# Two stages and a prologue: maxima taken in an earlier stage, and loads put in another order

## What is computed

```python
xn = layernorm(x)
q, k, v = rope(proj(xn, W_q)), rope(proj(xn, W_k)), proj(xn, W_v)
scores = einsum('bhnd,bhmd->bhnm', q, k) / sqrt(8)
attn = softmax(where(causal, scores, -inf), axis=-1)
s = einsum('bhnm,bhmd->bhnd', attn, v) -> (b, s, 128) @ W_o
g = silu(ffn(xn))                   # gelu(xn @ W1' + b1) @ W2' + b2
x = x + s * g
xn = layernorm(x)
x = x + retention(xn) * silu(mixture_of_experts(xn))
```

## Time and profile before

| what | us |
|---|---|
| median of 3 runs (1002.06 to 1005.51) | 1004.39 |
| the profiled execution, its own time | 999.11 |
| its span | 997.3 |
| first stage | 0 to 118.6 |
| attention's prologue | 118.6 to 149.4 |
| attention's loop | 149.4 to about 541 |
| between the layers | about 541 to 645 |
| retention, routing, experts | about 645 to 997 |

### The profile page before, as it was taken

One profiled execution on the slowest core, in us unless ns is written; L12 is line 12 of the kernel. 1 busy time (PEld: TensorE's weight loads), 2 busy tenths in 40 slices (PEclk: granted clock), 3 DMA queues, 4 the chain that ended last, 5 costly groups with the idle time before them and its releaser, 6 DMA issues. The chain is left out here.

```text
span 997.3 us, 25279 instructions
## 1 busy us (share of the span) xinstructions
PE 869.6 (87%) x9413; PEld 467.9 (47%) x9414; DVE 801.1 (80%) x1691; ACT 726.1 (73%) x1493; POOL 290.6 (29%) x335
## 2 busy tenths in 40 slices
PE   3999899999999999999988699888899999889960
PEld 3666544333334333333334577643444444468850
DVE  6665499999999999999942565399999999928895
ACT  2656408888888888888866445488999999948851
POOL 4875311111111000000012657600444443005560
PEclk9999959999999999999989799969999999979985
DMA  5579861644444353332005678596555443546627
GB/s 168 197 266 333 289 161 42 207 102 101 105 104 107 71 134 83 79 70 41 14 8 145 201 230 230 179 225 143 104 113 90 112 90 54 136 143 206 206 106 254
DMA packets 119385, 140.92 MB, mean 141 GB/s; under 512 B 20109, under 2 KB 82138, under 8 KB 118624
## 3 DMA queue, kind: packets, MB, share of 16 engines
q1 hardware_dynamic: 113888, 127.45, 46.5%
q0 software_dynamic: 5376, 11.85, 4.1%
HBM read 77.63 MB, written 63.25 MB: 141 GB/s over the span
## 5 line engine op out<-in xcount | busy, mean ns | idle before, releaser
L905 ACT ACTIVATE probsB<-psB 128x512 f32<-128x512 f32 (+2 forms) x640 | 310.1, 564 | 87.2 <-PE psB L979 60.1
L815 DVE TENSOR_REDUCE mxB<-psB 128x1 f32<-128x512 f32 (+2 forms) x448 | 257.0, 644 | 10.1 <-PE psB L943 8.4
L972 PE MATMUL psB<-q_groups,k_groups 64*128 64x512 bf16 (+3 forms) x768 | 206.3, 332 | 15.5 <-DVE mxB L815 8.3
L943 PE MATMUL psB<-k_groups,q_groups 64*128 64x512 bf16 (+3 forms) x768 | 216.8, 343 | 3.0 <-PEq L343 1.7
L1010 PE MATMUL psB<-probsB,vB 128*32 128x512 f32 (+3 forms) x1536 | 165.3, 502 | 0.7 <-ACT probsB L905 0.5
L1821 ACT ACTIVATE psD<-psD 128x896 f32<-128x896 f32 (+2 forms) x192 | 153.6, 800 | 8.7 <-PE psD L1875 8.5
L972 PEld LDWEIGHTS psB<-q_groups,k_groups 64*128 64x128 bf16 x768 | 67.5, 94 | 161.0 <-ACT probsB L905 141.2
L1750 DVE TENSOR_REDUCE sumsD<-psD 128x1 f32<-128x128 f32 (+3 forms) x256 | 113.4, 483 | 7.1 <-PE psD L1898 4.9
L1875 PE MATMUL psD<-k_groups,q_groups 64*128 64x512 bf16 (+3 forms) x384 | 103.5, 343 | 13.8 <-ACT psD L1821 5.6
L950 PE MATMUL psB<-hideB,chooseB 64*128 64x128 bf16 (+1 forms) x1024 | 115.1, 210 | 0.0
L815 DVE TENSOR_REDUCE mx2B<-psB 128x1 f32<-128x384 f32 (+2 forms) x192 | 104.6, 596 | 8.5 <-PE psB L950 6.4
(11 more groups left out here) (233 smaller groups left out, 1531.9 us busy)
## 6 DMA issues: line engine op xcount, KB each, us to landing
v<-vaugA SPq DMA_DIRECT2D x4, 2048.0 KB, 8.7
vB<-v SPq DMA_DIRECT2D x16, 512.0 KB
q_groups<-q SPq DMA_DIRECT2D x32, 200.0 KB
k_groups<-k SPq DMA_DIRECT2D x32, 200.0 KB
back<-emptyB POOLq DMA_DIRECT2D x16, 256.0 KB, 3.8
q<-hiA SPq DMA_DIRECT2D x12, 256.0 KB, 6.7
k<-hiA SPq DMA_DIRECT2D x12, 256.0 KB, 5.7
q_groups<-q SPq DMA_DIRECT2D x32, 96.0 KB
```

Source lines behind the costliest of these rows:

```text
L815: nc.vector.tensor_reduce(dst, src, AX.X, ALU.max).then_inc(max_read, 1)
L905: nc.scalar.activation(probs[:, n % DEEP, 0:w], st[n % BANKS][:, 0:w], ACT.Exp, scale=DH ** -0.5).then_inc(exp_done, 1)
L943: ins = nc.tensor.matmul(bank[:, to:to + w], q[half[r], s, hq // 2, t * P:t * P + P], k[half[r], s, hq // 2, HALF * c:HALF * c + w], start ...
L972: ins = nc.tensor.matmul(bank[:, to:to + w], k[half[r], s, hq // 2, jt * P:jt * P + P], q[half[r], s, hq // 2, i0:i0 + w], start=True, sto ...
```

## The change

1. `Groups` takes over the filling and reading of units (`fill_maximum`, `read_maximum`), and the first 24 units of group 0 (`EARLY`) move into the last feed-forward of the first stage. TensorE does them in pairs, with two heads side by side, in banks 0, 1, 4 and 5: one pair ahead of each quarter of the 16 matmuls of both halves, and one ahead of each of the four matmuls of the second half's hidden layer. VectorE reads 12 of them ahead of the first half's bias and 12 ahead of the second's. The attention's prologue starts at unit 24, and `empty` is cleared after unit 39.
2. At the attention's start SP loads q and k of group 2, then v of groups 0 to 2, then places the negated maxima of group 0, then loads group 3.
3. Between the layers `load_heads` for batch 2 is issued right after the last heads are stored, ahead of the load of den. It waits for three stores of rden and not for the fourth.
4. `residual` computes the variance plus epsilon and the negated mean on VectorE; GpSimd's `deviation` begins with the power.

```diff
+EARLY = 24
+    def fill_maximum(self, nc, s, unit, bank, done):
+        heads, t, c = unit
+        w, (choose, hide, _) = max_width(t, c), self.masks
...
+    def read_maximum(self, nc, par, unit, bank):
...
 (project_and_ffn, VectorE)
-                for half in range(2):
-                    add_bias(B - 1, half)
+                def read_early(first, last):
+                    for n in range(first, last):
+                        dve.wait_ge(groups.max_done, n + 1)
+                        groups.read_maximum(nc, 0, MAX_UNITS[n], early_banks[n % 4]).then_inc(groups.max_read, 1)
+                read_early(0, EARLY // 2)
+                add_bias(B - 1, 0)
+                read_early(EARLY // 2, EARLY)
+                add_bias(B - 1, 1)
 (project_and_ffn, TensorE)
+                def two_maxima(n):
+                    if n == 0:
+                        pe.wait_ge(groups.masks_loaded, 48)
+                        pe.wait_ge(groups.loaded[0], 64)
+                    if n == 2:
+                        pe.wait_ge(terms_ready, 2 * B)
+                    if n >= 4:
+                        pe.wait_ge(groups.max_read, n - 2)
+                    side_by_side(*(groups.fill_maximum(nc, 0, MAX_UNITS[i], early_banks[i % 4], groups.max_done) for i in (n, n + 1)))
                     for c in range(FC):
+                        if b == B - 1 and half == 1:
+                            two_maxima(8 + 2 * c)
...
                     for t in range(4):
+                        if b == B - 1:
+                            two_maxima(16 * half + 2 * t)
 (attention, SP)
-                load(0)
-                for x in range(1, QUADS):
-                    load(x)
+                groups.load_first(sp, A, 0, GROUPS_AHEAD)
+                for x in range(GROUPS_AHEAD + 1):
+                    load_values(x)
                 sp.wait_ge(max_read, place_of[0, None] + 1)
                 place(0)
+                for x in range(GROUPS_AHEAD + 1, QUADS):
+                    groups.load_first(sp, A, 0, x)
+                    load_values(x)
 (attention, VectorE and TensorE)
-                for n, (x, g) in enumerate(order):
-                    if n == AHEAD:
+                for n, (x, g) in list(enumerate(order))[EARLY:]:
+                    if n == EARLY + AHEAD:
...
-                for x, g in prologue:
+                for x, g in prologue[EARLY:]:
 (between_layers, SP)
                 kept_until.wait_heads(sp)
+                sp.wait_ge(g["rden_stored"], 16 * (B - 1))
+                sp.wait_ge(g["head_ready"], 4)
+                second.load_heads(sp, A, 2)
...
-                        if b == 0:
-                            load_heads(b + 2)
 (between_layers, VectorE and GpSimd)
+                    dve.wait_ge(g["moments"], at(NT, NT))
+                    nc.vector.tensor_scalar(var[:, :], mom[:, :, 1], LN_EPS, None, ALU.add).then_inc(g["var_ready"], 1)
+                    nc.vector.tensor_scalar(shift[:, :], mom[:, :, 0], -1.0, None, ALU.mult).then_inc(g["shift_ready"], 1)
...
-                    pool.wait_ge(g["moments"], at(NT, NT))
-                    nc.gpsimd.tensor_scalar(shift[:, :], mom[:, :, 0], -1.0, None, ALU.mult).then_inc(g["shift_ready"], 1)
-                    nc.gpsimd.tensor_tensor(var[:, :], mom[:, :, 1], eps[:, :], ALU.add).then_inc(g["var_ready"], 1)
```

109 lines of the change are left out of this document (55 added, 54 removed).

## The result

The changed kernel took **990.17 us** in the median of four runs (987.30 to 993.03), against 1003.37 for four runs of the kernel before, measured with it: a ratio of 0.987, interval 0.983 to 0.990. A second set of six runs gave a ratio of 0.985 (0.981 to 0.989). Over all ten the median is 989.5 us, so the change brings some 14 to 15 us. The forecast was 984.5, in a range of 981.0 to 990.5, with faster at 0.97. The direction is right and the time lies in the range, 0.3 us inside its upper end. It is 3.7 us above the 981.5 to 986.5 that had 0.55: about 5 us of the 19.9 that were forecast are missing.

The account below looks back on a forecast made before the run. No engine alone bounds the whole; waits in each stage do. Terms -12.9 + 1.5 + 0.7 - 9.2 = -19.9 take 999.11 to 979.2, with 0.5% added 984.5 us; range 981.0 to 990.5, with 981.5 to 986.5 at 0.55.

Parts of the forecast that it names:

- The prologue's reads: Attention's prologue: 24 maxima reads by VectorE move into the first stage, all on the path; -12.9 us.
- The tail: End of the first stage: the moved pairs and reads nearly fit into idle time; +1.5 us, bounds 0 and +5.0.
- with 0.3 for a pair: First stage's tail: five pairs of units behind TensorE's gelu wait cost 0.3 us each, 1.5 us in all.
- the tail pays: Rival, chance 0.13: pairs and reads in the first stage don't overlap, +5.0 in place of +1.5, 988.0 us.
- The place: Attention's start: placed negated maxima wait behind loads in SP's queue; +0.7 us, bounds 0 and +3.
- The clock: TensorE's clock stays low from the border until about 5 us after the loop's start, as before; zero, +-1.
- The third part: Between the layers, first batch: earlier load of third batch's heads removes VectorE's wait; -9.2 us, bounds -7.0 to -9.5.
- The fourth part: Between the layers: variance and shift on VectorE let GpSimd's power start 0.3 earlier; 0 us, bounds -0.9 to +1.2.
- A shift this early stays whole: Whole kernel: the gain persists to the end, as both stages behind repeat a fixed period.
- the negated maxima land late: Rival, chance 0.10, at the attention's start: +3 in place of +0.7, 986.8 us.
- The third part gave 2 us back: Rival, chance 0.12: a transfer becomes the bound in the next batch between the layers, 4 us back, 988.5 us.
- Slower, as the low clock stays: Rival, chance 0.03: low clock stays until about 188 where 143 is expected; 1008 us.

Follow-up runs that it names:

- old_order: Changed kernel with all four head groups' loads and v ahead of the placed negated maxima; 994.13 us, ratio 0.991.
- gpsimd_var: Changed kernel with variance and shift back on GpSimd (fourth part undone); 987.35 us, ratio 0.985.
- scale_behind_sums: Changed kernel, third group's v behind placed maxima, variance and shift on GpSimd, third batch's heads scaled behind first batch's state steps; 987.65 us.
- after: The changed kernel with all four parts, against the kernel before; 990.17 us (ratio 0.987), in a second set 988.49 us (0.985).
- before_heads_first: Kernel before with the third part alone: third batch's heads loaded ahead of the load of den; 996.41 us, ratio 0.992.
- heads_late: Changed kernel with the third batch's heads loaded behind the store of rden again (third part undone); 996.46 us, ratio 0.992.

## Why the prediction was right or wrong

**The prologue's reads** (-12.9 forecast): right. Border to cast 26.25 to 13.66, so -12.6.

**The tail** (+1.5 forecast, +3.5 found): the step that failed is "with 0.3 for a pair", together with "that wait covers all pairs of units put ahead of it". A pair costs 0.47 us: twelve of them cost 3.5 us net, with 2.2 us of gelu wait under them (3.5 + 2.2 = 5.7, by twelve), and four of them 1.93 by experiment. I had taken 0.34 for two matmuls and left out the small masking ones behind them, which eight of the twelve pairs have (0.25, partly side by side), and that a quarter takes longer when other matmuls stand beside it (1.10 from its first matmul to the next pair, where it took 1.03). Seven pairs at 0.47 are 3.3 us, more than the 2.2 that they could hide under. The mechanism was right: TensorE bounds this stretch, VectorE is just full. The rival "the tail pays" (+5.0) put it down to reads that don't overlap, and that isn't what happened. Its bound counted six late pairs, where the sum has five.

**The place** (+0.7 forecast, +0.8 and +0.9 in the two profiles, up to +1.4 in others with the same loads): right, and old_order shows why the second part is needed. The size has some luck in it. "TensorE ready some 0.5 us earlier" misread the rows: in the kernel before TensorE was busy with units until 0.08 us ahead of the loop's first matmul, so the 5.3 was no transfer time. In the changed kernel the wait is 1.23 and TensorE's own part 0.35 shorter, which leaves 0.8. The runs now settle what the trace of before could not say: 12.07, 6.2 and 5.00 us with less and less ahead of the transfer. The Trainium skill's page "DMA: Bandwidth & Descriptors", section "Queues, rings and completion order", says that each DMA engine takes the descriptors of a ring in the ring's order. The runs agree: with more ahead, the small transfer's first packet starts later behind its issue (0.7, 1.7 and 3.7 us).

**The clock** (0, +-1): right at this place. It is 0.50 from 130 to 135 in the prologue, still 0.50 from 145 to 146, and 0.89 from 146 to 147, nearly 6 us behind the loop's start, where before it rose 5 us behind it:

```profile
145.00:146.00 1.00, 1.00 (x8) 0.08 (x8) 0.68 (x2) 0.48 (x1) 0.00 (x0) 0.50 0.77 191
146.00:147.00 1.00, 1.00 (x24) 0.49 (x22) 0.00 (x0) 0.00 (x0) 0.00 (x0) 0.89 0.16 40
```

In the second profile of the changed kernel it rose 3 us behind the loop's start (140.66), so the point isn't fixed:

```profile
143.00:144.00 1.00, 1.00 (x20) 0.62 (x16) 1.00 (x3) 1.00 (x3) 0.00 (x0) 0.75 1.11 167
```

The forecast had no clock term between the layers, and there it should have had one.

**The third part** (-9.2 forecast; between -6 and -8 found): a term that was mis-sized, in three steps. "They start at 560.89, so the projection comes at 566.05": the sums' start didn't stay, it moved from 19.62 to 20.68 us behind the stage's entry, 0.7 by the scaling that now runs beside GpSimd's sums (19.66 without that overlap, 20.38 with it) and 0.3 by the fourth part. "The sums start at 594.19 and the next projection at 599.35, so 5.16": in the first batch it was 5.95 and 5.52. The 5.16 was right for a clock of 1.00: from the first sum to the projection it is 4.96 in gpsimd_var and 4.89 in scale_behind_sums, at 0.99 and 1.00, 5.95 at 0.82 in after, and 6.56 at 0.73 in before_heads_first. The sign "the projection 5 us behind the chunk sums with the clock at 1.00" wasn't seen in after, and was in those two. Stretches from the sums to the projection, in gpsimd_var and in before_heads_first:

```profile
555.70:560.70 5.00, 5.00 (x44) 4.87 (x44) 2.04 (x7) 3.31 (x4) 4.39 (x5) 0.99 1.03 357
```

```profile
562.90:569.50 6.60, 6.60 (x44) 6.47 (x44) 2.04 (x7) 4.01 (x5) 5.99 (x7) 0.73 1.03 372
```

The third step: "the chain of sums behind the stall also went slower" priced 10.4 us from one profile, where another execution of the same kernel needs 9.4 (565.50 to 574.87) and heads_late 8.6 (561.03 to 569.66). The first is a cost of the change, the second the clock of the execution, the last a base that was high. The third part is worth about 7 us: 6.2 to 6.9 over the whole stage by heads_late against the two profiles of after, 7.2 to 7.8 by before_heads_first against those of before, and 8.0 and 8.2 by the medians, whose intervals are wider than these differences.

**The fourth part** (0 forecast): about +1.1 by the profiles, of which 0.3 is shown, inside the bounds of -0.9 to +1.2. GpSimd's power does start 0.3 earlier, but the second half's rotary products on VectorE, and so the transposes and sums, start 0.3 later, and that chain is the one that ends last.

**The base.** "A shift this early stays whole" can't be seen in the first pair of profiles, which differ by 11.8 at the end. The second pair differs by 19.3. It holds by the medians: 15.1 us at the last batch between the layers (14.6 in the second pair), and 14 to 15 in time. The forecast had added 0.5% as the profiled execution was faster than the median; this was right, and the median over the later runs (1002.9 to 1004.6) confirms that base. The missing 5 us are 2.0 in the tail, some 2 in the third part and up to 1 in the fourth. All three misses go the same way, so no error hid another. The interval of the time is itself 7 us wide (0.983 to 0.990), so this sum rests on the profiles.

**The rivals.** That the negated maxima land late (+3) didn't come. The third part gave 2 us back, not by transfers in the next batch (before_heads_first: 23.34) but by the overlap on GpSimd and the clock. "Slower, as the low clock stays" fell: the clock came back 3 to 6 us behind the loop's start. Of the signs named, the border was at 120.7 (120 forecast, 122 the bound), the cast at 134.1 (132.5), the first exponential at 141.3 (139), TensorE's wait on the placed maxima 1.23 (2 the bound), no wait on the heads' scale or on den. The second batch, 24.49, was longer than its 24.05, for which the fourth part and the clock are candidates; 23.3 to 25.4 occur among the thirteen profiles, and 25.33 in the kernel before itself.

What stays open: why the granted clock comes back at different points of the same code, in the chain of sums, in the retention (236.23 against 230.16) and perhaps behind the experts' spread. The runs show that it does, not why.

## What to carry to other kernels

Work that is put into the idle time of one engine has to be paid on every engine that feeds it: here VectorE's 13 idle us took the reads as forecast, and TensorE, which had only 2.2 us to spare, paid 0.47 us for each pair. Price all instructions of such a unit, the small masking ones and the slowdown of what they are put between. When a wait goes away, ask beside which other work its successor now falls. And take the base from several executions: two stages that the change didn't touch differed by 6 and 5 us between profiles, more than any term but two.

## What the runs showed of the hardware

GpSimd's rotary sum of 128x512 floats takes 1.27 us, and 1.71 to 1.78 while VectorE scales the heads at the same time; the longer one was there in every execution with that overlap, and gone where the overlap was taken away (2.50 us for two). It costs VectorE as well: of its two products beside the sums (2.35 us together at 549.12) the first took 0.68 us and the second 1.75, where both take 0.68 or 0.69 at the stage's start. The early stages repeat as exactly: the tail took 14.37, 15.96 or 17.89 us and nothing between. The place does not: with the same loads in the same order it took 5.00 to 5.71, and 6.14 to 6.73. SP's issue of a small transfer took 1.2 us with 0.8 MB of q and k and 1.5 MB of values ahead of it and 6.12 with 1.3 MB more: the issuing engine was held, and not only the transfer. That a full queue held it is the likely reading; no run shows how full the queue was.
